# A fused Mamba-2 and LoRA-mixture block on one core: seven of its B tiles are turned by transposing DMAs instead of TensorE

## The reference, cut to what matters

```python
xn = layernorm(x)                                  # x: 1 x 1024 tokens x 512
proj = xn @ in_proj_w.T                            # gate 8192 | hs 8192, B 1024, C 1024 | dt 128
hBC = silu(causal_conv4(hs, B, C) + conv_b)
dt = clip(softplus(dt + dt_bias), 0, 100);  A = -exp(A_log)
# 128 heads of 64 channels, 8 groups of B and C of 128 states, 8 chunks of 128 tokens
Y_diag = (C B^T * L) (hs dt)                       # inside a chunk, L = exp(segsum(dt A))
states = B^T (decay * hs dt)                       # one state a head and chunk: B is used turned here
Y_off  = exp(A_cum) * C @ carried state
y = (Y_diag + Y_off + D hs) * silu(gate)
out = rmsnorm_per_group(y) * norm_w @ out_proj_w.T
return x + out + moe_lora(xn)                      # 512 x 512 base, 8 experts of rank 16, top 2
```

## Time and profile before

| | |
|---|---|
| median of 3 runs | 1624.7 us (1621.6 to 1625.2) |
| the profiled execution's own time | 1625.3 us |
| its span | 1624.0 us |
| busy: PE / DVE / POOL / ACT | 1601.9 / 1371.1 / 1337.9 / 1253.0 us |
| weight loads (PEld) | 1305.4 us |
| share of the chain that ended last | PE 90%, DVE 4%, POOL 2%, issue 2% |
| DMA queue of SP | 234 MB, 50.3% of 16 engines' span |

### The profile page before, as it was taken

One profiled execution on the slowest core, in us unless ns is written; L12 is line 12 of the kernel. 1 busy time (PEld: TensorE's weight loads), 2 busy tenths in 40 slices (PEclk: granted clock), 3 DMA queues, 4 the chain that ended last, 5 costly groups with the idle time before them and its releaser, 6 DMA issues.

```text
span 1624.0 us, 31886 instructions
## 1 busy us (share of the span) xinstructions
PE 1601.9 (99%) x10792; PEld 1305.4 (80%) x10792; DVE 1371.1 (84%) x1665; ACT 1253.0 (77%) x2643; POOL 1337.9 (82%) x1240
## 2 busy tenths in 40 slices
PE   8998999999999999999999999999999999999999
PEld 7776888888888888888888888888888888888777
DVE  5978789887988879898798978988798887989788
ACT  5177787887878788787877878788787878778774
POOL 3157689996899879898799968999688987999796
PEclk9999999999999999999999999999999999999999
DMA  4162355554555554444645446545564465645453
GB/s 134 54 209 97 116 170 179 164 150 134 158 156 140 163 156 146 124 143 139 192 148 138 125 139 186 150 134 150 150 165 119 130 167 161 177 121 133 133 163 105
DMA packets 216387, 236.12 MB, mean 145 GB/s; under 512 B 154273, under 2 KB 155809, under 8 KB 212001
## 3 DMA queue, kind: packets, MB, share of 16 engines
q1 hardware_dynamic: 216224, 234.07, 50.3%
HBM read 147.51 MB, written 55.05 MB: 125 GB/s over the span
## 4 chain that ended last, share of the span: by engine, by line
PE 90%; DVE 4%; POOL 2%; issue 2%; ACT 1%; DMA 0%; SPq 0%; POOLq 0%; DVEq 0%; ACTq 0%
PE P L268 8%; PE P L269 8%; PE P L270 8%; PE P L514 8%; PE P L364 7%; PE P L347 7%; PE P L365 7%; PE P L371 7%; PE P L354 7%; PE P L348 7%; PE P L379 4%; PE P L500 2%; PE P L497 1%; PE P L498 1%; PE P L488 1%
## 5 line engine op out<-in xcount | busy, mean ns | idle before, releaser
L624 ACT ACTIVATE P<-AB,SC 128x128 f32<-128x128 f32 x1008 | 303.9, 360 | 20.6 <-DVE EM L1018 20.5
L268 PE MATMUL P<-xh,AH 128*128 128x512 f32 x656 | 263.4, 401 | 1.7 <-DVE hsX L887 1.5
L887 DVE SCALAR_TENSOR_TENSOR hsX<-P,cwt,hsX 128x1023 f32<-128x1023 f32 x189 | 241.7, 1279 | 26.8 <-ACT hsX L555 22.3
L269 PE MATMUL P<-xl,AH 128*128 128x512 f32 x656 | 256.9, 392 | 0.0
L270 PE MATMUL P<-xh,AL 128*128 128x512 f32 x656 | 256.8, 391 | 0.0
L347 PE MATMUL P<-GH,xh 128*128 128x512 f32 x512 | 211.7, 413 | 0.0
L364 PE MATMUL P<-OH,gTh 128*128 128x512 f32 x508 | 199.4, 392 | 2.5 <-issue 2.4
L348 PE MATMUL P<-GH,xl 128*128 128x512 f32 x512 | 200.8, 392 | 0.0
L365 PE MATMUL P<-OH,gTl 128*128 128x512 f32 x508 | 197.8, 389 | 0.0
L1245 POOL TENSOR_TENSOR AL<-AR,AH 128x512 fp32r<-128x512 f32 x82 | 110.3, 1345 | 80.6 <-ACT AH L542 80.6
L1274 POOL TENSOR_TENSOR DL<-dxh,DH 128x512 fp32r<-128x512 f32 x112 | 173.3, 1547 | 0.0
(11 more groups left out here) (229 smaller groups left out, 4174.8 us busy)
## 6 DMA issues: line engine op xcount, KB each, us to landing
AB<-acr_d SPq DMA_DIRECT2D x128, 512.0 KB, 4.7
half_d<-hsX SPq DMA_DIRECT2D x60, 512.0 KB, 3.7
AR<-in_wa SPq DMA_DIRECT2D x80, 256.0 KB, 2.7
TS<-in_wg SPq DMA_DIRECT2D x16, 1024.0 KB, 5.2
TS<-in_wo SPq DMA_DIRECT2D x16, 1024.0 KB, 6.7
part_d<-pl SPq DMA_DIRECT2D x64, 256.0 KB, 3.2
pl<-part_d SPq DMA_DIRECT2D x64, 256.0 KB, 3.6
SC<-sct_d SPq DMA_DIRECT2D x16, 128.0 KB, 5.2
```

The source lines that it names most:

```text
L268: te.matmul(o, ah_, bh_, start=(first and i == 0), stop=False)
L269: te.matmul(o, ah_, bl_, start=False, stop=False)
L624: r = se.activation(decays(m)[:, h, :], AB[m % 2][:, h, :], ACT.Relu, bias=SC[s % 2][:, c, 3, h:h + 1], scale=-1.0)
L887: ve.scalar_tensor_tensor(out=o[:, d:T], in0=raw[:, 0:T - d], scalar=cwt[:, n, 3 - d:4 - d], in1=o[:, d:T], op0=ALU.mult, op1=ALU.add).the ...
```

## The change

B of steps 2, 4, ..., 14 is turned in the way of the H tiles. Its tile gets the two copies of its 16-bit planes into `low_high` (now also for "B" tiles: `turned` lists all turned tiles and `turn_no` numbers them), one store to a new buffer `bhalf_d`, and in each of the eight chunks a second transposing DMA of 256 rows into one of two new buffers `BT`, right behind that of `HT` on SP's queue and counted on the same semaphore. `nht` gives the count for which the readers of `HT` and `BT` wait, so in an even step each of them waits for both transfers. TensorE's transposition stays for step 0 alone. `BH` and `BL` are made from `BT`, and what waited for the BG bank before reading the turned piece waits for the DMA (`BH`), while the masked product `Gt` gets the wait for the bank for itself.

```diff
+    turned = [i for i, t in enumerate(ctiles) if t[0] == "H" and t[1] or t[0] == "B" and t[1]]
+    turn_no = {i: n for n, i in enumerate(turned)}
...
+    def nht(m):
+        return 16 * sum(2 if n // 8 % 2 == 0 else 1 for n in range(m, 7, -2))
...
+        BT = [sb(f"BT{i}", [128, 128]) for i in range(2)]
...
-                te.transpose(o[:, 0:128], Bx[:, tok(c)], ident[:, :])
+                if s == 0:
+                    te.transpose(o[:, 0:128], Bx[:, tok(c)], ident[:, :])
                 te.matmul(o[:, 128:256], Bx[:, tok(c)], Cx[:, tok(c)], start=True, stop=True).then_inc(s_bg, 1)
...
-                se.wait_ge(s_bg, ngc(m))
+                if s:
+                    se.wait_ge(ht_in[m % 2], nht(m))
+                    se.wait_ge(s_x, 1 + tile_no["C", s])
+                else:
+                    se.wait_ge(s_bg, ngc(m))
...
-                se.activation(BH[:, c, :], bank("BG", m)[:, 0:128], ACT.Copy).then_inc(s_bh, 1)
+                se.activation(BH[:, c, :], BT[m % 2][:, :] if s else bank("BG", m)[:, 0:128], ACT.Copy).then_inc(s_bh, 1)
...
-                ve.tensor_tensor(BL[:, c, :], o[:, 0:128], as_f(BH[:, c, :]), ALU.subtract).then_inc(s_bl, 1)
+                ve.tensor_tensor(BL[:, c, :], BT[m % 2][:, :] if s else o[:, 0:128], as_f(BH[:, c, :]),
+                                 ALU.subtract).then_inc(s_bl, 1)
+                ve.wait_ge(s_bg, ngc(m))
...
-                ve.wait_ge(ht_in[m % 2], 16 * (m // 2 - 3))
+                ve.wait_ge(ht_in[m % 2], nht(m))
...
+            t = ctiles[i]
+            sp.dma_start(half_d[t[1] % 2, t[2]] if t[0] == "H" else bhalf_d, low_high).then_inc(half_st[n % 4], 16)
...
             sp.dma_start_transpose(HT[m % 2].bitcast(u16), rows[:, tok(c)]).then_inc(ht_in[m % 2], 16)
+            if s % 2 == 0:
+                sp.wait_ge(s_bl, ngc(m) - 2)
+                rows = bhalf_d.rearrange("p b t -> (p b) t")
+                sp.dma_start_transpose(BT[m % 2][:, :].bitcast(u16), rows[:, tok(c)]).then_inc(ht_in[m % 2], 16)
```

More of the change, by code:

```diff
@@ L20, in mamba_moe_block_kernel @@
     half_d = nc.dram_tensor("half_d", [2, 4, 128, 2, T], u16, kind="Internal").ap()
+    bhalf_d = nc.dram_tensor("bhalf_d", [128, 2, T], u16, kind="Internal").ap()
     eal_d = nc.dram_tensor("eal_d", [NS, 8, NC], f32, kind="Internal").ap()
@@ L107, in nsa, with turns_of @@
         return 6 * (m // 8) + m % 8
+    turned = [i for i, t in enumerate(ctiles) if t[0] == "H" and t[1] or t[0] == "B" and t[1]]
+    turn_no = {i: n for n, i in enumerate(turned)}
+    def turns_of(s):
+        return sum(1 for i in turned if ctiles[i][1] <= s)
+    def nht(m):
+        return 16 * sum(2 if n // 8 % 2 == 0 else 1 for n in range(m, 7, -2))
     ctx = ExitStack()
@@ L286, in turned_no @@
         def turned_no(i):
-            t = ctiles[i]
-            return 4 * (t[1] - 1) + t[2] if t[0] == "H" and t[1] else None
+            return turn_no.get(i)
         tanh5 = (EM[1][:, 0:512], th[:, 512:1024])
@@ L547, in act_tap @@
             se.wait_ge(s_half, 2)
-            if t[0] == "H" and t[1] and turned_no(i) > 1:
-                se.wait_ge(s_hi, turned_no(i) - 1)
-                se.wait_ge(s_lo, turned_no(i) - 1)
+            if t[0] == "H" and t[1]:
+                p_ = tile_no.get(("H", t[1] - (t[2] < 2), (t[2] + 2) % 4))
+                if p_ in turn_no:
+                    se.wait_ge(s_hi, turn_no[p_] + 1)
+                    se.wait_ge(s_lo, turn_no[p_] + 1)
             elif t[0] != "H" and t[1] > 0:
@@ L554, in act_tap @@
                 se.wait_ge(s_cl, 4 * t[1])
+                if t[1] > 2 and t[0] == "B":
+                    se.wait_ge(s_lo, turn_no[tile_no["B", t[1] - 2]] + 1)
             se.activation(tile_out(i), pair("A", i), ACT.Identity, bias=cbt[:, n:n + 1], scale=cwt[:, n, 3:4]).then_inc(s_tap, 1)
@@ L1263, in pool_scaled @@
             if s:
-                pe_.wait_ge(ht_in[m % 2], 16 * (m // 2 - 3))
+                pe_.wait_ge(ht_in[m % 2], nht(m))
             else:
@@ L1412, in sp_halves @@
             sp.wait_ge(s_lo, n + 1)
-            sp.dma_start(half_d[(n // 4 + 1) % 2, n % 4], low_high).then_inc(half_st[n % 4], 16)
+            t = ctiles[i]
+            sp.dma_start(half_d[t[1] % 2, t[2]] if t[0] == "H" else bhalf_d, low_high).then_inc(half_st[n % 4], 16)
         def sp_turned(m):
@@ L1417, in sp_turned @@
             if c == 0:
+                n_ = turns_of(s)
                 for j in range(4):
-                    sp.wait_ge(half_st[j], 16 * s)
+                    sp.wait_ge(half_st[j], 16 * ((n_ + 3 - j) // 4))
             sp.wait_ge(s_dhs, m - 1)
```

## The result

The changed kernel takes 1634.0 us (median of 5 runs, 1632.1 to 1634.8) against 1624.7 us (median of 5 runs, 1621.6 to 1625.4), a ratio of 1.0059 with an interval of 1.0047 to 1.0070. The forecast was 1621.0 us with a range up to 1627.5 us: the sign is wrong and the time lies outside the range. The profiled execution took 1634.8 us, its span is 1633.5 us, 9.5 us more than before.

The account below looks back on a forecast made before the run. TensorE, busy 99% of the span, was taken as the bound. Saving 4.3 us less 0.4 for `BL` and 0.2 for the second DMA gave 3.7 us, so 1621.0 us against the median; range 1617.5 to 1627.5 us.

Parts of the forecast that it names:

- the term for `BL`: VectorE's `BL` with both sources in SBUF: 0 to 0.28 us more each, taken as 0.05 each, 0.4 us in all.
- Rival 2: VectorE's chain from c = 1 to c = 3: longer `BL` eats the gain, about 1624.5 us; chance 0.2.
- TensorE's saving: On TensorE, 56 transpositions removed at 0.11 us each; 39 of them reach the end, 4.3 us saved.
- Rival 1: On TensorE, each removed transposition gives back up to its busy 0.27 us: 10.5 us, 1614 us; chance 0.13.
- the windows that shorten: In even steps, the windows after Y of 8s + 1 to 8s + 5 were to shorten by 0.11 us.
- The wait at c = 1: TensorE's wait for `Gt` in iteration 8s was to grow from 0.15 to about 0.4 us.
- The copies, the store and `BH`: Two copies per tile on ScalarE and GpSimd, the tile's store, and `BH` reading SBUF: costed at nothing.
- The second DMA: `BT`'s transposing DMA on SP's queue: 0.5 us of queue, landing 2.6 us after issue, 0.2 us lost in all.
- my place of danger: c = 5 (chunk 53 in step 6), where `BT` was to land about 0.4 us after `BH` would start, without loss.
- rival 3: Late second DMA stalls output product O at c = 5: 1628 us, behind more traffic 1635; chance 0.13.
- The rule that I weighed: Skill advice to turn 128 x 128 on TensorE if PSUM will do; by it rival 3 would be the rule.

Follow-up runs that it names:

- the run with that part alone: Kernel before, with TensorE's transposition left out from step 2 on and nothing in its place, `BH` and `BL` made from another PSUM piece: 1619.7 us, ratio 0.9974.

## Why the prediction was wrong, step by step

**The step that failed** is the term for `BL`: "By that ratio `BL` costs 0 to 0.28 us more ... I take 0.05 each, 0.4 us, for it is short." It cost 0 to 1.10 us more, 0.73 us in the mean of the 56 (1006 against 279 ns), and its effect at the end is 12.8 us in the kernel before and 15.2 us between the changed kernel and the one with `BL` from PSUM. It was not only a size. I had read from `dxh` (0.69 us alone, 1.35 us in step 6) that such an operation gets longer by a factor, so that a short one pays little. The 0.69 us were not even taken alone: in the trace of before GpSimd's `xch` starts 0.05 us behind that `dxh` and runs beside it to its end. It is `xch` that gets longer there, 1.55 us where it can take 1.04 us, for it came second:

```profile
553.57 1.55 POOL L1270 TENSOR_TENSOR xch<-hsX,SC 128x512 f32<-128x512 f32 x1 [0.59 <-DMA hsX<-half_d]
```
The mechanism is a wait for an instruction under way; then the short one pays as much as the long one, since the price is what is left of the neighbour. The trace of before could have told. GpSimd's row beside the `dxh` of the earlier trace rows, which I had not looked at, and GpSimd beside a `BL` at c = 2 (timeline of the kernel before):

```profile
743.11 1.03 POOL L1259 COPY hsX<-hsX 128x1024 uint16<-128x1024 uint16 x1
```

```profile
709.72 1.77 POOL L1390 TENSOR_TENSOR hsX<-hsX,pl 128x512 f32<-128x512 f32 x1
710.25 0.28 DVE L991 TENSOR_TENSOR BL<-P,BH 128x128 fp32r<-128x128 f32 x1
```

That copy ends at 744.14, and `dxh` at 743.34 + 1.35 = 744.69, 0.55 us later; all eleven `dxh` that I lined up between 650 and 796 us end 0.54 to 0.56 us behind a GpSimd instruction. That is a wait with a fixed remainder, not a ratio. And the sum beside `BL` (L1390) had 1.24 us left at its start: that, and not 0.28 us, was the upper bound.

**Where it went.** Rival 2 named the mechanism's place, VectorE's chain from c = 1 to c = 3, and gave it 2.6 + 1.5 us by the same small bound. In the chunks c = 2, 3 and 4 of step 6 `BL` took 1.37, 0.53 and 1.13 us, together 2.19 us more than 3 x 0.28 us, in a chain with a slack of 0.52 us whose engine was busy for 11.44 of 11.61 us. The window of 50 grew by 0.93 us. From the end of one `Gt` (c = 1) to the end of that of c = 4 VectorE's rows balance: `BL` +2.20 us, `OL` (L928) +0.46 us and L934 +0.25 us, which meet GpSimd at other moments, and `dxh` -0.97 us, together +1.9 us; 0.9 us of it is taken from idle time (1.9 us before, 1.0 us after), and the stretch grew by 1.1 us (34.49 to 35.57 us), twice its slack. `dxh` got shorter at c = 2 above all, 0.72 us (from 712.24) where it took 1.69 us before (from 708.64), as the GpSimd instruction that it now meets (L1266, to 712.40) is nearly over; the next one, L1411, then holds up `BL` instead. The stalls at c = 0 and c = 1 are worth 0.66 and 0.48 us a step. That at c = 0 I had not listed at all, for I looked for slack only with VectorE unchanged; and at c = 1 I had let a longer `BL` cost up to 2 us over the seven steps, where the places c = 0 and c = 1 now take 7 x 1.14 = 8 us.

**TensorE's saving**: right. From the start of the last gate product to the second product of the next half tile, 0.80 us before, it is now 711.25 - (709.88 + 1.08 - 0.39) = 0.68 us, where I had said 0.69:

```profile
709.88 1.08 PE L365 MATMUL P<-GL,xh 128*128 128x512 f32 x4
710.80 0.38 PE L349 MATMUL P<-Cx,Bx 128*128 128x128 f32 x2
710.94 0.48 PE L279 MATMUL P<-xh,AH 128*128 128x512 f32 x1
711.25 0.40 PE L280 MATMUL P<-xl,AH 128*128 128x512 f32 x1
```

What reaches the end was 4.3 us by my sum and 4.5 us by the run with that part alone (interval 2.6 to 6.0). Rival 1, up to 10.5 us, falls: each of the windows of 48 to 53 got shorter by 0.10 us, not by 0.27 us. One label was off: the windows that shorten are those of 8s to 8s + 5 (c = 2 to 7), and I had left out 8s. The wait at c = 1, 0.15 us before, was to become 0.4 us; it is 0.56 us.

**The copies, the store and `BH`**: nothing, as said. The copies of B take 1.05 us on ScalarE and 1.04 us on GpSimd.

**The second DMA**: no loss, as said, with one input off. From the view of the tile (ns min, median, max of the time on SP's queue; then the landing):

```profile
L1451 SPq DMA_TRANSPOSE BT<-bhalf_d x56: 1230/1234/1914, 292.8 to 1528.4; - x56
...
DMA to landing us min/median/max: 2.4/2.9/4.7
```

The landing, 2.9 us in the median, is near the 2.6 us that I took. The queue time is 1.23 us, not 0.5 us and just above my bound of 1.2 us. At chunk 53, my place of danger, `HT` is issued at 739.71 and lands 5.4 us later, at 745.1; `BT` lands 0.3 us behind it, and `BH`, held up by the rest, starts only 1.6 us after that:

```profile
742.62 1.24 SPq L1451 DMA_TRANSPOSE BT<-bhalf_d  x1
...
747.05 0.30 ACT L626 ACTIVATE BH<-BT 128x128 fp32r<-128x128 f32 x1
```

The changed kernel as a whole can't tell this, since everything there is late; the run with `BT` made but unused can, and shows no loss with the deadlines of the kernel before. The 0.2 us that I took for it lies below what that run can tell. The stall of rival 3 does come up in the run with `BL` on GpSimd, in four steps.

**The rule that I weighed.** I had set the advice of the Trainium skill, page "VectorE: DVE Perf Modes", Rules for kernel authors, to turn 128 x 128 on TensorE where PSUM will do, against the change, for the sake of the DMA's landing. The kernel did get slower, but not by that: with `BL` back on PSUM the turn by DMA is the faster one (1618.8 against 1624.2 us). What PSUM as the destination gave here was a VectorE operand that GpSimd cannot hold up.

**Sum.** -4.5 us (TensorE) + 12.8 us (source of `BL`) + 0 us (DMA side) = +8.3 us, against 9.3 us measured; the difference is within the intervals of the parts. The parts need not add up, though. By the windows of step 6 they are -0.61 us and +1.87 us, 1.26 us together, and the changed kernel has 1.57 us: what TensorE saves ahead of a late `Gt` it waits away.

## What to carry to other kernels

When a change moves an operand of a VectorE instruction from PSUM to SBUF, count its SBUF sources: with two, it waits in full for the GpSimd instruction that was under way first (here all of these read SBUF), so its price is what is left of that instruction and not a share of its own length. If it comes first, GpSimd waits instead, so a start a few hundredths of a us earlier or later can be worth 1.1 us. Price it chunk by chunk from GpSimd's rows at that place, and look at whether VectorE has idle time there before relying on another order. Keeping one source in PSUM, by a spare ScalarE copy if need be, can be cheaper than either.

## What I had not expected of the hardware

- The held up instruction ends a fixed time after the one that it waited for, whatever this is (for `BL`: L1411, L1291, L1320, L1280, L1271), and that time is 0.13 to 0.15 us less than it takes when it isn't held up: 0.05 us behind for 32 columns (0.18 us by itself), 0.15 us for 128 (0.28 us), 0.55 us for the 512 of `dxh` (0.69 us), 1.08 us for the 1024 of L934 (1.22 us). On GpSimd it is 1.15 us for its sums (1.30 us) and 0.90 us for `xch` (1.04 us).
- Either engine can be the one that waits. With starts 0.02 us apart or less it was VectorE in two steps and GpSimd in others of one and the same execution.
- The transposing DMA of 256 rows keeps SP's queue as long as the one of 1024 rows does when that is free: 1.23 us against 1.16 us.
- `BH` from SBUF takes ScalarE 0.30 us, against 0.27 us from PSUM.
